# A recurrent attention layer and an eight-expert layer: row lists kept per sequence, and twelve expert tiles placed around the last sequence

## Time and profile before

| | us |
|---|---|
| median of 3 runs | 679.05 (678.91 to 683.32) |
| the profiled execution | 674.16 |
| its span, first to last instruction | 672.3 |
| PE busy in the span | 593.8 (88%) |
| DVE, ACT, POOL busy | 343.8, 280.1, 226.1 |
| mean granted clock | 0.952 of full speed |

### The profile page before, as it was taken

One profiled execution on the slowest core, in us unless ns is written; L12 is line 12 of the kernel. 1 busy time (PEld: TensorE's weight loads), 2 busy tenths in 40 slices (PEclk: granted clock), 3 DMA queues, 4 the chain that ended last, 5 costly groups with the idle time before them and its releaser, 6 DMA issues.

```text
span 672.3 us, 12520 instructions
## 1 busy us (share of the span) xinstructions
PE 593.8 (88%) x3638; PEld 501.2 (75%) x3639; DVE 343.8 (51%) x864; ACT 280.1 (42%) x671; POOL 226.1 (34%) x384
## 2 busy tenths in 40 slices
PE   3979999999999999977632799999999999999992
PEld 2547676777768677766421799999999999999992
DVE  2395968879595959677147123322322332332331
ACT  3554667575676767552430232223223223223220
POOL 6614262515334351611122122233233233233221
PEclk9999999999999999979665799999999999999997
DMA  9900014141302212020222964455455455455300
GB/s 325 402 12 1 0 33 95 32 94 33 83 12 75 53 32 64 33 63 33 63 63 86 347 232 179 175 217 205 172 203 218 168 202 218 179 189 225 119 29 2
DMA packets 26844, 83.48 MB, mean 124 GB/s; under 512 B 3437, under 2 KB 13039, under 8 KB 20656
## 3 DMA queue, kind: packets, MB, share of 16 engines
q1 hardware_dynamic: 21120, 67.98, 30.4%
q0 software_dynamic: 4992, 14.45, 5.8%
q10 hardware_dynamic: 688, 0.52, 0.2%
HBM read 70.33 MB, written 13.52 MB: 125 GB/s over the span
## 4 chain that ended last, share of the span: by engine, by line
PE 71%; DVE 9%; issue 4%; ACT 2%; POOL 1%; DMA 1%; DVEq 0%; ACTq 0%; POOLq 0%
PE bank_a L1133 21%; PE bank_c L1147 20%; PE bank_l L889 5%; PE bank_a L901 4%; PE bank_c L1003 4%; PE bank_a L930 3%; DVE arena L1198 2%; DVE arena L1209 2%; PE bank_b L981 2%; PE bank_a L946 2%; PE bank_a L939 2%; PE bank_b L980 1%; PE bank_b L1121 1%; PE bank_b L967 1%; PE bank_c L1020 1%
## 5 line engine op out<-in xcount | busy, mean ns | idle before, releaser
L1463 DVE TENSOR_TENSOR arena<-bank_a,b_col 128x512 f32<-128x512 f32 x78 | 54.0, 692 | 189.5 <-PE bank_a L1133 175.7
L1133 PEld LDWEIGHTS bank_a<-masks,arena 128*128 128x128 f32 x1248 | 147.0, 194 | 1.9
L1133 PE MATMUL bank_a<-masks,arena 128*128 128x128 f32 x1248 | 147.1, 277 | 0.0
L1147 PE MATMUL bank_c<-w_sb,arena 128*128 x624 | 141.5, 380 | 1.4 <-ACT arena L864 0.9
L1147 PEld LDWEIGHTS bank_c<-w_sb,arena 128*128 128x128 f32 x624 | 115.5, 190 | 16.4 <-issue 2.3
L889 PEld LDWEIGHTS bank_l<-arena,k_mix 128*128 128x128 f32 x448 | 65.2, 197 | 47.2 <-ACT k_mix L685 34.6
L1198 DVE TENSOR_TENSOR arena<-arena 128x256 f32<-128x256 f32 x224 | 89.6, 442 | 9.3 <-PE bank_l L889 9.3
L864 ACT ACTIVATE arena<-arena 128x512 f32<-128x512 f32 x78 | 45.0, 622 | 107.4 <-PE bank_c L1147 102.9
L889 PE MATMUL bank_l<-arena,k_mix 128*128 128x128 f32 x448 | 72.9, 288 | 14.2 <-DVE arena L1209 12.2
L854 ACT ACTIVATE masks<-bank_b,b_col,g_col 128x128 f32<-128x128 f32 x78 | 31.4, 453 | 129.1 <-PE bank_b L1121 129.1
L901 PE MATMUL bank_a<-arena 128*128 128x512 f32 x160 | 81.9, 611 | 0.0
(11 more groups left out here) (137 smaller groups left out, 747.8 us busy)
## 6 DMA issues: line engine op xcount, KB each, us to landing
arena<-w SPq DMA_DIRECT2D x39, 1024.0 KB
routed_rows<-arena SPq DMA_DIRECT2D x8, 1026.0 KB, 7.8
arena<-x SPq DMA_DIRECT2D x16, 512.0 KB, 5.6
w_sb<-w SPq DMA_DIRECT2D x8, 1024.0 KB, 14.0
arena<-b SPq DMA_DIRECT2D x1, 1024.0 KB, 4.8
arena<-routed_rows,take_now POOLq DMA_INDIRECT x39, 4.1
out<-k_mix,put_now POOLq DMA_INDIRECT x39, 2.5
arena<-wk SPq DMA_DIRECT2D x1, 256.0 KB, 3.9
```

Of the source, the lines that this page charges most:

```text
L1133: m = pe.matmul(bank_a[k // 4][:, k % 4 * P:(k % 4 + 1) * P], w1_now[t.par][:, i * F + k * P:i * F + (k + 1) * P], xl_t[t.par % 2][:, i * ...
L1147: m = pe.matmul(bank_c[p][:, 0:D], h_act[:, k * P:(k + 1) * P], w2_sb[:, bass.ds(e * (FC * D) + k * D, D)], start=(k == 0), stop=(k == FC ...
L1463: dve.tensor_tensor(h_sb[:, n * 512:(n + 1) * 512].rearrange("p (k t) -> p k t", t=P), bank_a[n][:, :].rearrange("p (k t) -> p k t", t=P), ...
```

## The change

Five things are changed.

1. **Lists by expert.** After the affinities of each sequence, DVE runs `route` (6 small operations) at the end of the step. In the next step PE runs `ranks` (2 matmuls, after the second matmul group of level 0) and DVE `slots` (2 small operations, after level 1). POOL's `list_rows` turns the slots into integers and writes each row's number to a DRAM list `rows_by_expert`, in its expert's region, by four indirect DMAs of 128 single numbers.
2. **Tables in two parts.** `early_tables` (22 small DVE operations, one of them waiting for the other) in step 7 lays out 12 tiles that are full, from the rows of sequences 0 to 4. `last_tables`, in three parts between tiles 4 to 7, lays out the other 27.
3. **Gathers by two indirect DMAs.** `fetch_ids` reads a tile's 128 row numbers from the list, then `gather` takes the rows. `scatter` adds `skip` to the numbers. The old tables and the copies L648 and L658 go.
4. **Order.** `pipeline` ends with step 8. There SP loads `w1` for tiles 0 to 3, and POOL issues four `fetch_ids` and four `gather`s ahead of the output norm of the last sequence. On PE the transposes of `x1` come before the outputs, and the affinities go between them. What was step 9 (`o_transposes`, `out_proj`, `x1_transposes`, `affinity`, `ranks`) now stands between tiles 0 to 4. The wait that held the second `w1` load until two gathers had landed goes.
5. **Memory.** The attention weights move between the two halves of the double buffers, so that the first half and the weights can be overwritten by `w1`, the gathered rows and `b2` in step 8. The down matmuls write `bank_l` in place of `bank_c`. Three stores write rows of `w2` to the unwritten part of `routed_rows` in step 2, so that every row of it is defined.

The core of the diff:

```diff
...
-            for i in range(NSEQ + 2):
+            for i in range(NSEQ + 1):
...
+                    need(sp, s_o, 2, c, 2)
+                    need(sp, s_og, 2, c, 2)
+                    need(sp, s_state, 5, c, 5)
+                    need(sp, s_dz, H, b, H)
+                    need(sp, s_q0, 1, b, 1)
+                    for n in range(SLOTS):
+                        fetch_w1(tile(n))
...
+            def store_rows(c):
+                if number(c) == EARLY:
+                    sp.wait_ge(s_defined, 16 * (NSEQ - EARLY))
+                need_apart(sp, s_zn, TJ, c, TJ)
+                need_apart(sp, s_base, TJ, c, TJ)
+                need_apart(sp, s_alpha, 1, c, 1)
+                sp.dma_start(seq_rows(rows_t, c), tiles(row_sb, RW)).then_inc(s_row_out, 16)
...
-            sp.wait_ge(s_idx, 3)
-            rounds(sp, turn)
+            pipeline(sp, step)
+
+            sp.dma_start(b2_sb, b2.rearrange("e f -> (e f)").partition_broadcast(P)).then_inc(s_b2, 16)
+            for n in range(SLOTS, SLOTS + 3):
+                fetch_w1(tile(n))
+            store_rows(LAST_SEQ)
+            for n in range(SLOTS + 3, NA):
+                fetch_w1(tile(n))
+            rounds(sp, fetch_w1)
...
+            def list_rows(c):
+
+                n = number(c)
+                need(pool, s_slot, 2, c, 2)
+                pool.tensor_copy(slot_i[:, n * TJ:(n + 1) * TJ], slot_f[:, n * TJ:(n + 1) * TJ]).then_inc(s_sloti, 1)
+                need_apart(pool, s_sloti, 1, c, 1)
+                for j in range(TJ):
+                    t = n * TJ + j
+                    pool.indirect_dma_start(out=listed, out_offset=bass.IndirectOffsetOnAxis(ap=slot_i[:, t:t + 1], axis=0),
+                                            in_=ids[:, t:t + 1], in_offset=None).then_inc(s_listed[n >= EARLY], 16)
+
             def step(a, b, c, nxt):
...
+                if a is None:
+
+                    pool.wait_ge(s_listed[0], 16 * TJ * EARLY)
+                    pool.wait_ge(s_idx, 2)
+                    for n in range(SLOTS):
+                        fetch_ids(n)
+                    need(pool, s_o, 2, c, 2)
+                    need(pool, s_state, 5, c, 5)
+                    pool.wait_ge(s_row_out, 16 * EARLY + 16)
+                    for n in range(SLOTS):
+                        gather(n)
                     need(pool, s_on, TJ, b, 0)
                     norm("o", b)
...
+                    if c is not None and number(c) > 0:
+                        list_rows(before(c, 1))
...
+            def fetch_ids(n):
+
+                pool.indirect_dma_start(out=id_of[:, n:n + 1], out_offset=None, in_=listed,
+                                        in_offset=bass.IndirectOffsetOnAxis(ap=take_idx[:, n:n + 1], axis=0)).then_inc(s_ids[n % SLOTS], 16)
+
+            def gather(n):
+                p = n % SLOTS
+                pool.wait_ge(s_ids[p], 16 * (n // SLOTS) + 16)
+                need(pool, s_yo, 1, Step(n // SLOTS - 1, p, SLOTS), 1)
+                pool.indirect_dma_start(out=gathered[p], out_offset=None, in_=rows,
+                                        in_offset=bass.IndirectOffsetOnAxis(ap=id_of[:, n:n + 1], axis=0)).then_inc(s_rows[p], 16)
+
+            def scatter(n):
+                p = n % SLOTS
+                pool.tensor_tensor(put_of[:, n:n + 1], id_of[:, n:n + 1], skip[:, n:n + 1], ALU.add).then_inc(s_put, 1)
+                pool.wait_ge(s_put, n + 1)
+                need(pool, s_yo, 1, Step(n // SLOTS, p, SLOTS), 1)
+                pool.indirect_dma_start(out=out, out_offset=bass.IndirectOffsetOnAxis(ap=put_of[:, n:n + 1], axis=0),
+                                        in_=y_out[p], in_offset=None, bounds_check=N - 1, oob_is_err=False).then_inc(s_out[p], 16)
+
+            def turn(n):
+                if n + SLOTS < TILES:
+                    gather(n + SLOTS)
+                scatter(n)
 
...
+            list_rows(LAST_BUT_ONE)
+            for n in range(SLOTS, 2 * SLOTS):
+                fetch_ids(n)
+            double_norm(LAST_SEQ)
+            for n in range(3):
+                turn(n)
+                fetch_ids(n + 2 * SLOTS)
+            list_rows(LAST_SEQ)
+            turn(3)
+            fetch_ids(3 + 2 * SLOTS)
+            turn(4)
+            turn(5)
+            pool.wait_ge(s_idx, 5)
             pool.wait_ge(s_row_out, 16 * NSEQ + 16)
-            pool.wait_ge(s_idx, 3)
...
+            gains(tile(0))
+            gains(tile(1))
+            for j in range(TJ):
+                o_norm(LAST_SEQ, j)
+            relu(tile(0))
+            for i in range(DC):
+                o_copy(LAST_SEQ, i)
+            gains(tile(2))
+            turn(tile(1))
+            relu(tile(2))
+            x1_copies(LAST_SEQ)
+            gains(tile(4))
+            rows_of(LAST_SEQ)
+            turn(tile(3))
+            alphas(LAST_SEQ)
+            for n in range(4, NA):
+                turn(tile(n))
             rounds(act, turn)
...
+            def ranks(c):
+
+                need(pe, s_route, 6, c, 6)
+                need(pe, s_x1t, DC, c, DC)
+                if number(c) in (EARLY - 1, NSEQ - 1):
+                    pe.matmul(bank_c[1][:, E * TJ:E * (TJ + 1)], ones[:, :], upto5[:, :, TJ], start=True, stop=True).then_inc(s_total, 1)
+                pe.matmul(bank_c[1][:, 0:E * TJ], earlier, hot5[:, :, 1:TJ + 1], start=True, stop=False)
+                pe.matmul(bank_c[1][:, 0:E * TJ], ones[:, :], upto5[:, :, 0:TJ], start=False, stop=True).then_inc(s_rank, 1)
+
...
 
-                    of(b, outputs, 0)
-                    of(b, outputs, 1)
-                    of(c, x1_transposes)
-                    for n in range(DC * TJ):
-                        of(c, affinity, n)
+                    x1_transposes(c)
+                    outputs(b, 0, lambda n: affinity(c, n))
...
+            c = LAST_SEQ
+            need(pe, s_og, 2, c, 2)
+            z_transposes(tile(0))
+            z_transposes(tile(1))
+            need(pe, s_at0, H, c, H)
+            up(tile(0))
+            ranks(LAST_BUT_ONE)
+            o_transposes(c, 0)
+            o_transposes(c, 1)
+            pe.wait_ge(s_w2, 16 * E)
+            need(pe, s_pick, 2 * LEVELS, c, 2 * LEVELS)
+            turn(tile(0))
+            for half in range(2):
+                for j in range(2):
+                    out_proj(c, half, j)
+            turn(tile(1))
+            x1_transposes(c)
+            turn(tile(2))
+            for n in range(DC * TJ):
+                affinity(c, n)
+            turn(tile(3))
+            ranks(c)
+            for n in range(4, NA):
+                turn(tile(n))
             rounds(pe, turn)
...
+            def route(c):
+
...
+                need(dve, s_best, 1, c, 1)
+                dve.tensor_tensor(by_e(is_max), by_e(aff[:, :]), over_e(aff_best[:, :]), ALU.is_equal).then_inc(s_route, 1)
+                need(dve, s_route, 6, c, 1)
+                dve.scalar_tensor_tensor(out=by_e(is_max), in0=by_e(is_max), scalar=-float(E), in1=over_j(iota_e[:, :]),
+                                         op0=ALU.mult, op1=ALU.add).then_inc(s_route, 1)
+                need(dve, s_route, 6, c, 2)
+                dve.tensor_reduce(first, by_e(is_max), AX_X, ALU.min).then_inc(s_route, 1)
+
+                need(dve, s_rank, 1, c, 0)
+                need(dve, s_slot, 2, c, 0)
+                dve.tensor_copy(hot5[:, :, 0], upto5[:, :, TJ]).then_inc(s_route, 1)
+                need(dve, s_route, 6, c, 3)
+                dve.scalar_tensor_tensor(out=hot5[:, :, 1:TJ + 1].rearrange("p e j -> p j e"), in0=over_j(iota_e[:, :]),
+                                         scalar=-float(E), in1=over_e(first), op0=ALU.add, op1=ALU.is_equal).then_inc(s_route, 1)
+                need(dve, s_route, 6, c, 5)
+                dve.tensor_tensor_scan(out=upto, data0=carry, data1=hot, initial=0.0, op0=ALU.mult, op1=ALU.add).then_inc(s_route, 1)
...
+            def early_tables():
+
+                tile_counts(region_e, 0)
+                tile_experts(0, NA)
+                tile_rows(region_e, NA)
+                dve.tensor_scalar(take_idx[:, 0:NA], column_of(4, NA), row_at[:, 1:2], None, ALU.add).then_inc(s_idx, 1)
+
+                own(dve.tensor_scalar(t_upto, t_upto, float(NA), None, ALU.min))
+                own(dve.tensor_tensor(rest_e[:, 1:E], t_upto[:, 1:E], t_upto[:, 0:E - 1], ALU.subtract))
+                own(dve.tensor_copy(rest_e[:, 0:1], t_upto[:, 0:1]))
+                own(dve.scalar_tensor_tensor(out=rest_e, in0=rest_e, scalar=float(P), in1=region_e, op0=ALU.mult, op1=ALU.add))
...
+            def slots(c):
+
+                n = number(c)
+                need(dve, s_rank, 1, c, 1)
+                if n in (EARLY - 1, NSEQ - 1):
+                    dve.wait_ge(s_total, 1 + (n == NSEQ - 1))
+                    own(dve.tensor_copy(end_e, bank_c[1][:, E * TJ:E * (TJ + 1)]))
+                dve.tensor_tensor(by_e(place), bank_c[1][:, 0:E * TJ].rearrange("p (e j) -> p j e", e=E),
```

(50 more changed lines are left out.)

372 lines of the change are left out of this document (162 added, 210 removed).

## The result

The change made the kernel slower: **736.59 us** median (733.78 to 739.23) against 678.98 (678.75 to 683.32) for the kernel before on the same chip, a ratio of 1.0844 with a 95% interval of 1.081 to 1.0878. Forecast were 649 us and a range of 642 to 662. The profiled execution has a span of 732.0 us, where before had 672.3.

A forecast was written before the change was run, and what follows sets the result against it. PE was taken as the bound, its idle time from 289 to 373 us as the prize. Tile 6 came 36.2 us earlier, less 4.7 (steps 3 to 7) and 1.5 (step 8): 30 gained, 679.05 to 649, range 642 to 662.

The forecast's parts named there:

- the one on `list_rows`: Attention steps, POOL: four indirect DMAs at 1.3 us plus 0.3, 5.5 us in a gap of 9.41; cost 0.
- SP's three extra stores: Step 2: they wait for long-loaded weights and move 3 MB with DMA at 0.17 of capacity; cost 0.
- The first tile: After the outputs: PE idle about 7 us, starting at 327.1, with the first tile near 333.
- rival 2: Tile start: gathers wait behind four w1 loads, first tile 5 to 6 us later, gain 24, 655 us; chance 0.10.
- The attention steps: Steps 3 to 7: `route` and `slots` add 0.95 us each, bounds 0 and 1.65; 4.7 us in all.
- Rival 1: Attention: list DMAs stop DVE's `update`, or small operations cost in full; gain 17 to 25, 654 to 662; chance 0.17.
- `early_tables`: Step 7: 22 small DVE operations, 4.5 us, hidden where DVE idles 4.63 us for PE; cost 0.
- rival 3: Tiles: POOL's three indirect DMAs per tile become the bound, slower, 707 us at 3.0 us each; chance 0.03.
- rival 4: Tile start: late pieces of the last sequence hold the tiles behind them; gain 0 to 10, 669 to 679; chance 0.05.
- the rest of the sum: Step 8 to tile 6: its down matmuls start at 392.4 instead of 428.57, 36.2 us saved, less 1.5 for step 8.
- granted clock of 1.00: Tiles 0 to 8: no PE gap over 1 us and a granted clock of 1.00 there.
- All three signs of being wrong: Steps longer by over 1.7 us, gap ahead of tile 0 over 12, z transposes waiting for gathers in later tiles.

The follow-up runs named there:

- e3: The changed kernel without its 32 list writes, the table written once at the start with constant row numbers: 657.01 us, ratio 0.9716.
- e5: The changed kernel with its 4-byte list writes going to places 512 bytes apart: 657.47 us, ratio 0.9725.
- e2: The kernel before plus 20 scatters of 128 4-byte numbers into a table nobody reads, 16 neighbouring numbers per run: 733.72 us, ratio 1.0855.
- e11: The changed kernel with its 4-byte list elements 64 bytes apart: 660.13 us, ratio 0.9748.
- e9: e2 with the places of its scattered numbers 512 bytes apart: 678.76 us, ratio 1.0028 against the kernel before.
- e8: The changed kernel with list elements of 64 bytes instead of 4: 660.02 us, ratio 0.9736.
- e4: The changed kernel with list elements of 512 bytes instead of 4: 663.39 us, ratio 0.9831.
- e1: The changed kernel with each sequence's x load issued one step earlier, ahead of the row store: 690.22 us, ratio 1.0228.
- e6: The changed kernel with the edits of e4 and e1 together: 655.96 us, ratio 0.9694.
- e10: e5 plus the edit of e1, row lists of the first four tiles fetched early, third and fourth w1 loads held for two gathers: 645.77 us, ratio 0.9548.
- e13: e2 with each 64 bytes shared by 16 adjacent partitions instead of every eighth one: 769.74 us, ratio 1.1401.

## Why the prediction was wrong

**The step that failed is the one on `list_rows`**: "5.5, in a gap of 9.41: cost 0, and also at 1.8". It costed a DMA by what its issue takes on POOL, and that was right (starts 1.26 to 1.40 us apart). It had no term for the transfers themselves, which is the overlap that it had wrong: how long 128 numbers of 4 bytes take to land, and what else is on the 16 DMA engines meanwhile. The price was 76 us (e3, e5). No row of the kernel before shows a write of 4 bytes, and it should have been bounded from both sides as a transfer. The gather's landing of 4.1 us, a read of wide rows, stood only for the fetches; for the landing of the list writes (14.8 us), and for the store and the load beside them, nothing stood at all.

**Shown** is this: the writes alone make the loss (e2, ratio 1.0855 against 1.0844 for the whole change); without them, or with 64 bytes between them, the change is a gain (e3, e5, e11); the distance makes it, not size or count (e9 against e2; e8, e4). On the path it ends as a late `x` load (e1). Not shown is what the memory does with such writes; I only see DMA shares of 0.72 at 57 GB/s. The Trainium skill (DMA: Bandwidth & Descriptors, Specifications) says that below 512 B the DMA engines read, modify and write, and gives 512 B as the least size for full rate. The runs don't agree that the size alone sets the price: 4 bytes at 64 bytes' distance land in 2.2 us (e11), and e4's 512-byte elements gave the slower kernel of the two (0.9831 against 0.9725). The measurement decides; what collides within 64 bytes may still be such a read and write back, but no run shows it. The same page (Issuing engines are not separate DMA queues) says that DMAs of all engines share the 16 DMA engines and interleave; here the trace agrees, as POOL's writes brought SP's store from 7.8 to 18.8 us.

**"SP's three extra stores ... 0"** was wrong by 1 to 5 us: the step that holds them took 38.6 in e5 and 42.1 in e3 and e8, against 37.5, and 43.7 in the changed kernel, ahead of its first list write. I read the mean DMA share of 0.17, but the `x` load queued right behind 3 MB. One step of lead makes it 0 (e1, e6).

**The first tile** was forecast at a gap of 7 us; with the list writes harmless it was 13.29 (e5). Beside the four `w1` loads the fetches took 5.7 to 6.8 us to land, and the gathers 9.7 to 10.5, where I let each take 4.1. That is rival 2. Its "5 to 6 later" in all was nearly right (6.3), though its "3 us longer" was too much for the numbers and too little for the rows.

**The attention steps** were within the bounds once the transfers were harmless: 37.5 us in e5 and e10. I had read 36.31 as the length of a step, but that is the last one, which has no `x` load; the others took 37.0. So it is +0.5, where I took +0.95 with bounds of 0 and 1.65. Rival 1 falls. In steps 3 to 7 its premise does not come about: in e5 the four list DMAs of a step end at 181.46, and the next `update` begins at 182.90. In step 8 they do meet, and there the rule of the Trainium skill (SBUF — State Buffer, Who interferes with whom), held to the list DMAs, does not come out: beside them two `update`s (L1286, the L1198 of before) take 0.74 to 0.81 us, and in the same stretch of before, alone, 0.75 to 0.79.

```profile
305.37 0.96 POOL L631 DMA_INDIRECT rows_by_expert<-arena  x1 [0.30 <-issue]
305.48 0.74 DVE L1286 TENSOR_TENSOR arena<-arena 128x256 f32<-128x256 f32 x2
```

`early_tables` stayed hidden (36.65 us for the window 307.20 to 343.85). **POOL** is not the bound (rival 3): tiles run at 7.25 us with three indirect DMAs each.

**The new order** did most of what it was to do (rival 4 falls). The fair test of the rest of the sum is e5, the changed kernel with nothing but its places spread: 2.75% or 19 us gained, where I forecast 30 and gave 25 to 34. Its tile 6 is 9.1 us behind the forecast 398.6 (392.4 and the 6.2 of the steps):

```profile
338.07 0.66 PE L1184 MATMUL bank_b<-ident,arena 128*128 128x128 f32 x2 [13.29 <-DMA arena<-routed_rows,id_of]
...
390.19 0.44 PE L1184 MATMUL bank_b<-ident,arena 128*128 128x128 f32 x2 [3.01 <-DMA arena<-routed_rows,id_of]
391.05 5.40 PE L1212 MATMUL bank_l<-w_sb,arena 128*128 x16 [0.42 <-issue]
...
407.66 3.62 PE L1212 MATMUL bank_l<-w_sb,arena 128*128 x16
```

The first tile takes 6.3 of the 9.1 (13.29 less 7). From there to tile 6 it is 69.6 us where I had 65.3; the wait for the gather of tile 6, and the slower down matmuls behind it, are the 4.3. The steps give 1.5 back. e10 has tile 6 at 397.00 and gains 31 us, close to the forecast 30, but that is partly luck: it has three edits that the forecast kernel lacks, its first tile is 6 us earlier than forecast (327.24 against 333.3), and the 69.8 us from there to tile 6 are again over 4 too many. The forecast granted clock of 1.00 between the first tiles did not come either: 0.84 in the changed kernel, 0.93 in e10.

All three signs of being wrong that the prediction named did show: steps longer by more than 1.7 us, a gap ahead of tile 0 of over 12, and transposes that wait for gathers in later tiles. The slower side had 0.03, all of it on POOL's time per instruction. The rival that came true, transfers that hold each other up, was in the list only for the gathers and only with a gain left.

## What to carry to other kernels

A DMA has two prices: what its issue takes on the queue, and what its packets do to every other transfer in flight; cost both, the second for each load that stands behind it and for who waits for that load. Where a kernel scatters single 4-byte numbers, spread their places: 16 bytes apart still cost something here, 64 bytes apart nothing that these runs could tell; let the reader use the wider pitch. When an experiment cures a loss, ask which two things it changed, as e4 did here.

## What the hardware showed

- Twenty scatters of 128 numbers of 4 bytes, 16 numbers to 64 bytes, add 59 us (e2, every eighth partition), or 94 when the sharers are adjacent partitions (e13); 512 bytes apart they add 1.8 us (e9).
- Landing of such a scatter: 14.8 us at 4 bytes apart, 5.0 at 16, 2.2 at 64, 2.3 at 512. Beside it a store of 1 MB takes 18.8 us in place of 7.8, and the DMA share reads 0.72 at 57 GB/s: a high share is no sign of bytes moved.
- Reads of single 4-byte numbers from neighbouring places are not dear: the fetches landed in 3.0 us (median) even in the changed kernel, and in 2.5 with the numbers 512 bytes apart (e5).
- A late load costs twice: in two lengthened steps of e2 PE's busy time for the same work was 38.0 us at granted clocks of 0.87 and 0.84, against 35.9 at 1.00 before.
- Beside a list DMA of POOL, DVE's `update` with both inputs in SBUF took 0.74 to 0.81 us for two, as alone (e5); beside POOL's elementwise L602 it took 1.60.
